# Half of a pairwise sum of attention exponentials moved from GpSimd to an accumulating DMA

## The chip, the cores and the metric

The kernel runs on one core of a Trainium2 chip. The metric is the device time of one execution in microseconds, lower is better. The engines named below are TensorE (PE, its weight loads PEld), VectorE (DVE), ScalarE (ACT), GpSimd (POOL) and SyncE (SP, which here only issues DMAs). The 16 DMA engines of the core move the data of every queue: of SP's, and of POOL's own queue.

## The reference

A post-norm decoder layer in float32, batch 2, 1024 tokens, width 512, 16 heads of 32: linear self-attention, then cross-attention to a context of 2048 rows, then a mixture of 8 experts (top 2). The change touches the softmax of the cross-attention alone:

```
q = (x1 @ wq.T)   -> [b, 16, 1024, 32]
k = (x2 @ wk.T)   -> [b, 16, 2048, 32]
v = (x2 @ wv.T)   -> [b, 16, 2048, 32]
dots = einsum('bhnd,bhmd->bhnm', q, k) * SCALE
attn = softmax(dots, axis=-1)
out  = einsum('bhnm,bhmd->bhnd', attn, v)
```

## The kernel before

There are three stages: the linear attention and the projections of the context (until about 570 us), the attention loop (until about 1530 us), and the experts. A plan, made in Python by `do(stage, key)`, is one list of units; every engine walks the list and carries out its own part of each unit, in that order, so the order of each engine's queue is the order of the plan.

**The loop.** A group is 4 heads (HG = 4) of one batch element. A turn is one group and one half of the queries (512); there are 16 turns. A turn walks the 2048 context rows in MT = 16 tiles of 128, two tiles at a time, so it has 8 pairs and the loop has 128. For each tile `s` and head `j`, TensorE multiplies keys and queries (`score`, L1194), ScalarE writes `exp` into `probs_of(t, s)[:, j, :]` (L1807). An exponential tile is 128 partitions x 4 heads x 512 queries, 8 KB in each partition. Even tiles lie in a ring of three buffers `probs_sum`, odd ones in a ring of three `probs_add`. The numerators (`num`, L1205) multiply both tiles with the values. For the denominators, the two tiles of a pair are first added, `a += b` with a in `probs_sum` and b in `probs_add` (`add_pair`, L1929 to L1936, POOL, one instruction for each head), and one multiplication with ones sums the result (`den`, L1223). Besides, each pair computes 8 tiles of scores for the row maxima of a later turn (L1175), which DVE reduces (L1468). The last 12 pairs are added by DVE (`by_vector`) and are not touched.

**The order in one pair.** The plan of a pair (L844 to L892, one `clock` each) is: the 8 scores of the next pair mixed with 8 maxima, some side work, `num` of both tiles, `den` of the pair before (it was put in `pending` with `clock + 1`), postponed divisions, then `add_pair`. So TensorE meets the `den` of a pair one whole pair after POOL was told to add it. `add_pair` waits for the last exponential of the odd tile and for the numerators of the even one. ScalarE, before it overwrites a buffer three pairs later, waits for its `num_summed`, and for `den_summed` (even tiles) or `pair_added` (odd tiles).

**Other traffic.** SP loads, during the loop, the keys of a later group in four chunks of three 256 KB transfers (`load_k`, L2070), queries (`load_q`, three of 256 KB), values (`load_v`, four of 256 KB), and stores and fetches rows of 1 MB at the end of a half. POOL also does the divisions by the denominators (`divide`, L1957) and, in the stage of the experts, gathers rows (L1968) and scatters results with an accumulating indirect DMA (`down`, L1977: 128 rows of 2 KB added to rows in DRAM, 256 KB in all).

Of the kernel before, what the change touches and what calls it, by code (L numbers as in the profile page):

```python
# [12 lines left out]
ALU = mybir.AluOpType  # L13
# [6 lines left out]
HG = P // DH  # L20
# [4 lines left out]
MT = M // P  # L25
# [95 lines left out]
def program(nc, t):  # L121
    ctx = ExitStack()
    with ctx:
        def signal(name, by=1):
            return Signal(Semaphore(ctx.enter_context(nc.semaphore(name))), by)

        def signals(name, n, by=1):
            return [signal(f"{name}{i}", by) for i in range(n)]

        def signals_on(name, n):  # L130
            on = Semaphore(ctx.enter_context(nc.semaphore(name)))
            return [Signal(on) for _ in range(n)]
# [16 lines left out]
        def bank(i):  # L149
            return pairs[i // 2][:, i % 2, :]  # L150
# [131 lines left out]
        def by_vector(t, s):  # L282

            return t == LAST or t == LAST - 1 and s >= HALF_TURN

        def chunk_of(b, mc):
            return B * NH + b * MCH + mc

# [34 lines left out]
        max_scored, max_taken = signal("max_scored"), signal("max_taken")  # L323
        top_taken, inverted = signals_on("tops_inverses", 2)
        top_hi, shift_copied = signals_on("shift_parts", 2)
        shift_turned = signal("shift_turned")
        scored, exp_done = signal("scored"), signal("exp_done")
        num_summed, num_copied = signal("num_summed"), signal("num_copied")
        pair_added, divided, top_lo = signals_on("pool_done", 3)
        last_pair_added = signal("last_pair_added")  # L330
        den_summed, den_copied = signal("den_summed"), signal("den_copied")
        counts_zero, folded = signals_on("fold_done", 2)
# [64 lines left out]
            "score": lambda t, s, j: (scored, exp_done),  # L397
            "num": lambda t, s: (num_summed,),
            "copy_num": lambda t: (num_copied,),
            "add_pair": lambda t, s: (last_pair_added if by_vector(t, s) else pair_added,),  # L400
            "den": lambda t, s: (den_summed,),
            "copy_den": lambda t: (den_copied,),
            "invert": lambda t, q: (inverted,),
# [180 lines left out]
        def context(b):  # L584
            for mc in range(MCH):
                m = chunk_of(b, mc)
                load_chunk(m + 2)
                for u in range(NG):
                    i = main_bank.next()
                    take_bank(("ctx_k", b, mc, u), i)  # L590
                    do("ctx_k_first", b, mc, u)
                    yield
                    do("ctx_k", b, mc, u)
                    yield
                    i = main_bank.next()
                    take_bank(("ctx_v", b, mc, u), i)
                    do("ctx_v_first", b, mc, u)
                    yield
                    do("ctx_v", b, mc, u)
                    split_chunk(m + 1, u)  # L600
                    yield
# [239 lines left out]
        for turn, (n, h) in enumerate(turns):  # L841
            b, g = groups[n]
# [51 lines left out]
        b, h = B - 1, NH - 1  # L894
        for k in range(HT):
# [1 line left out]
            do("rows_first", b, h, k)  # L897
        begin_parts(b, h)
        loop_end = (scored, num_summed, den_summed, exp_done, num_copied, den_copied, pair_added, last_pair_added,
                    max_taken, shift_copied, max_scored)  # L900
        gates["experts"] = [x.now() for x in loop_end]
        while divisions:
            invert(SHARE, 0)
# [112 lines left out]
        def probs_of(t, s):  # L1016

            tiles = probs[s % 2]
            return tiles[(t * MT + s) // 2 % len(tiles)]

        def probs_before(t, s):

            earlier_step = t * MT + s - 2 * len(probs[s % 2])
            return divmod(earlier_step, MT) if earlier_step >= 0 else None
# [4 lines left out]
        def _(_eng):  # L1029
            pe = Waits(nc.tensor)  # L1030

            def free_bank(*unit):
                if held_before[unit]:
                    pe.wait_ge(*emptied(held_before[unit]))
                return bank(bank_of[unit])
# [104 lines left out]
            def ctx_k_terms(b, mc, u):  # L1140
                return three_passes(columns(w_parts["k"], tile_of(u)), src_parts[chunk_of(b, mc) % 2])

            def ctx_k_first(b, mc, u):
                out = free_bank("ctx_k", b, mc, u)
                pe.wait_ge(*chunk_lo[chunk_of(b, mc), NC - 1])
                pe.wait_ge(*weight_lo["cv", NC - 1])
                terms = ctx_k_terms(b, mc, u)
                accumulate(out, terms[:len(terms) // 2], stop=False)
# [61 lines left out]
            def denominators_of(t, s):  # L1210
                if s == 1:
                    free_bank("den", t)
                tiles = [probs_of(t, s - 1)]
                if t == LAST and s == MT - 1:
                    tiles.append(probs_of(t, s))
                    pe.wait_ge(*exp_done[t, s, HG - 1])
                elif by_vector(t, s):
                    pe.wait_ge(*last_pair_added[t, s])
                else:
                    pe.wait_ge(*pair_added[t, s])  # L1220
                for tile in tiles:
                    for j in range(HG):
                        done = nc.tensor.matmul(bank(DEN)[j * DH:(j + 1) * DH, :], ones[:, 0:DH], tile[:, j, :],  # L1223
                                                start=s == 1, stop=s == MT - 1 and tile is tiles[-1])
                done.then_inc(den_summed.sem, 1)
# [72 lines left out]
            def down(e, i):  # L1298
# [3 lines left out]
                for f in range(NF):  # L1302
# [7 lines left out]
                    "turn_heads": turn_heads, "project": project, "turn_x1": turn_x1, "xq": xq,  # L1310
                    "ctx_k_first": ctx_k_first, "ctx_k": ctx_k, "ctx_v_first": ctx_v_first, "ctx_v": ctx_v,
                    "max": max_scores, "shift": shift, "score": score, "num": numerators, "den": denominators_of,
                    "rows_first": rows_first, "rows": rows, "parts_first": parts_first, "parts": parts,
                    "x1_logits": x1_logits, "fold": fold, "fold_turn": fold_turn, "logits": logits, "ranks": ranks,
# [388 lines left out]
        def _(_eng):  # L1703
            act, S = Waits(nc.scalar), nc.scalar
# [91 lines left out]
            def score(t, s, j):  # L1796
                act.wait_ge(*scored[t, s, j])
                if j == 0 and probs_before(t, s):
                    t0, s0 = probs_before(t, s)
                    act.wait_ge(*num_summed[t0, s0])  # L1800
                    if s0 % 2 == 0:
                        act.wait_ge(*den_summed[t0, s0 + 1])
                    elif by_vector(t0, s0):
                        act.wait_ge(*last_pair_added[t0, s0])
                    else:
                        act.wait_ge(*pair_added[t0, s0])
                S.activation(probs_of(t, s)[:, j, :], bank(bank_of["score", t, s, j]), ACT.Exp, scale=SCALE) \  # L1807
                    .then_inc(exp_done.sem, 1)

# [64 lines left out]
            def final(q):  # L1874
# [3 lines left out]
                for n in range(Q4):  # L1878
# [10 lines left out]
                    "split_chunk": split_chunk, "split_weight": split_weight, "keys": keys, "queries": queries,  # L1889
                    "turn_heads": turn_heads, "turn_x1": turn_x1, "xq": xq, "ctx_k": ctx_k, "ctx_v": ctx_v,  # L1890
                    "shift_high": shift_high, "shift": shift, "score": score, "copy_num": copy_num, "copy_den": copy_den, "x2": x2,
                    "x1_logits": x1_logits, "fold": fold, "parts": parts, "route_top": route_top, "turn_xe": turn_xe,
                    "split_w1": split_w1,
# [8 lines left out]
        def _(_eng):  # L1902
            pool, G = Waits(nc.gpsimd), nc.gpsimd
# [25 lines left out]
            def add_pair(t, s):  # L1929
                if not by_vector(t, s):  # L1930
                    a, b = probs_of(t, s - 1), probs_of(t, s)
                    pool.wait_ge(*exp_done[t, s, HG - 1])
                    pool.wait_ge(*num_summed[t, s - 1])
                    for j in range(HG):
                        done = G.tensor_tensor(a[:, j, :], a[:, j, :], b[:, j, :], ALU.add)  # L1935
                    done.then_inc(pair_added.sem, 1)  # L1936

# [34 lines left out]
            def down(e, i):  # L1972
                turn = e * NS + i
                pool.wait_ge(*eo_ready[e, i])
                if turn:
# [4 lines left out]

            here = {"gate_loop": pass_gate, "gate_second": pass_gate, "gate_experts": pass_gate, "gate_tail": pass_gate,
                    "load_consts": load_consts, "fetch_x": fetch_x, "shift_low": shift_low, "add_pair": add_pair,
                    "store_x1": store_x1, "divide": divide,
                    "gather": gather, "down": down}
# [244 lines left out]
```

## Time and profile before

| | us |
|---|---|
| median of 2 runs | 2080.24 (2080.16 to 2080.32) |
| the profiled execution's own time | 2077.41 |
| its span, first to last instruction | 2075.6 |
| busy: PE / DVE / ACT / POOL | 1931.0 / 1228.6 / 889.2 / 784.8 |
| first to last pair sum on POOL (L1935) | 570.1 to 1456.4 |

The span is 1.8 us shorter than the time of its own execution. A busy engine is not by itself the bound: what counts is which engine the others wait for at a given place, which the waits and the chain of a stretch tell. "issue" as a releaser is time in which an engine waited for nothing that the profile shows. The time from issue to landing of a DMA is counted from the start of the issuing instruction to the last update of its semaphore.

### The profile page before, as it was taken

What the parts mean: (1) busy time and instruction counts of PE and PEld (TensorE: products, weight loads), DVE (VectorE), ACT (ScalarE), POOL (GpSimd) and SP (SyncE); (2) the same over time, 40 slices, a digit from 0 to 9 for tenths busy, and PEclk for the clock granted to TensorE, in tenths of its full rate; (3) what the DMA queues carried; (4) which work ended last, traced back from release to release, by engine and by line L of the source; (5) the groups of instructions that cost most, each with busy time, mean ns of one, the idle gap of its engine ahead of it and who ended that gap; (6) DMA issues with size and microseconds to landing.
All of it is one profiled execution on the core that took longest, in us unless ns stands there. A gap on an engine that the chain in (4) does not pass through costs nothing.

```text
span 2075.6 us, 26469 instructions
## 1 busy us (share of the span) xinstructions
PE 1931.0 (93%) x10152; PEld 1270.0 (61%) x10152; DVE 1228.6 (59%) x2321; ACT 889.2 (43%) x1595; POOL 784.8 (38%) x675
## 2 busy tenths in 40 slices
PE   6999999999499999999999999999978999999991
PEld 5876666677355555555444544544438998888991
DVE  5565453157277777777767866877753444444434
ACT  3212322222265666656545545545734433333432
POOL 4002200000076777777656656756102222222110
PEclk9999999999799999999999999999988999999996
DMA  7002524574603122312424334332224444544315
GB/s 254 28 1 107 177 81 147 190 212 137 156 17 78 25 73 57 92 42 58 97 62 121 79 77 118 84 80 72 82 82 143 137 132 99 135 132 104 100 21 177
DMA packets 118942, 211.03 MB, mean 102 GB/s; under 512 B 10480, under 2 KB 28544, under 8 KB 118736
## 3 DMA queue, kind: packets, MB, share of 16 engines
q1 hardware_dynamic: 107264, 183.30, 30.0%
q0 software_dynamic: 9440, 21.86, 5.5%
q10 hardware_dynamic: 2112, 4.19, 0.5%
q8 instruction: 80, 1.31, 0.3%
q14 instruction: 46, 0.38, 0.1%
HBM read 147.15 MB, written 62.42 MB: 101 GB/s over the span
## 4 chain that ended last, share of the span: by engine, by line
PE 78%; DVE 13%; DMA 4%; ACT 2%; SPq 1%; issue 1%; POOL 0%; POOLq 0%; DVEq 0%; ACTq 0%
PE banks L1039 33%; PE banks L1205 11%; PE banks L1294 11%; PE banks L1175 9%; DVE max L1468 9%; PE banks L1194 7%; PE banks L1223 5%; PE banks L1045 2%; ACT probs_sum L1807 1%; DMA y_rows<-eo,tok 1%; DMA k_parts<-out_lo 1%; DMA wv_raw<-in_wv_t 1%; DMA bxo_cols<-in_bxo_cols 1%; DVE stats L1677 0%; DMA k_half<-in_xwk_t 0%
## 5 line engine op out<-in xcount | busy, mean ns | idle before, releaser
L1468 DVE TENSOR_REDUCE max<-banks 128x1 f32<-128x512 f32 x1024 | 628.1, 681 | 188.6 <-PE banks L1175 187.9
L1935 POOL TENSOR_TENSOR probs_sum<-probs_sum,probs_add 128x512 f32<-128x512 f32 x464 | 582.1, 1286 | 351.6 <-PE banks L1205 351.6
L1175 PE MATMUL banks<-k_stack,q_stack 98*128 98x512 f32 x1024 | 428.9, 426 | 30.4 <-DVE max L1468 30.0
L1807 ACT ACTIVATE probs_sum<-banks 128x512 f32<-128x512 f32 x512 | 264.9, 604 | 330.1 <-PE banks L1194 329.4
L1194 PE MATMUL banks<-q_stack,k_stack 98*128 98x512 f32 x1024 | 378.0, 400 | 15.2 <-ACT probs_add L1807 14.7
L1175 PEld LDWEIGHTS banks<-k_stack,q_stack 98*128 98x128 f32 x1024 | 192.3, 188 | 220.0 <-DVE max L1468 99.6
L1807 ACT ACTIVATE probs_add<-banks 128x512 f32<-128x512 f32 x512 | 271.7, 612 | 0.6 <-PE banks L1194 0.5
L1194 PEld LDWEIGHTS banks<-q_stack,k_stack 98*128 98x128 f32 x1024 | 192.4, 189 | 76.4 <-ACT probs_add L1807 26.0
L1977 POOL DMA_INDIRECT y_rows<-eo,tok x40 | 79.9, 1998 | 217.7 <-DVE eo L1667 163.6
L1205 PE MATMUL banks<-probs_sum,v_grp 128*32 128x512 f32 x1024 | 142.5, 618 | 0.0
L1205 PE MATMUL banks<-probs_add,v_grp 128*32 128x512 f32 x1024 | 139.5, 606 | 0.0
L1223 PE MATMUL banks<-probs_sum,ones 128*32 128x512 f32 x1024 | 137.4, 599 | 0.8 <-DVE probs_sum L1483 0.8
L1654 DVE TENSOR_TENSOR hid_lo<-hid,hid_hi 128x640 fp32r<-128x640 f32 x64 | 52.8, 825 | 142.5 <-ACT hid_hi L1872 142.5
L1039 PE MATMUL banks<-w_hi,hid_hi 128*128 128x512 f32 x320 | 128.6, 402 | 0.0
L1039 PE MATMUL banks<-w_hi,hid_lo 128*128 128x512 f32 x320 | 126.3, 395 | 0.0
L1039 PE MATMUL banks<-w_lo,hid_hi 128*128 128x512 f32 x320 | 125.8, 393 | 0.0
L1941 POOL TENSOR_TENSOR x_nat<-x_nat,bxo_row 128x512 f32<-128x512 f32 x16 | 21.1, 1350 | 267.7 <-PE banks L1045 267.7
L1294 PE MATMUL banks<-xe_hi,w_hi 128*128 128x320 f32 x512 | 117.6, 311 | 1.5 <-issue 1.5
L1294 PE MATMUL banks<-xe_lo,w_hi 128*128 128x320 f32 x512 | 117.3, 310 | 0.0
L1294 PE MATMUL banks<-xe_hi,w_lo 128*128 128x320 f32 x512 | 117.2, 310 | 0.0
L1867 ACT ACTIVATE hid<-banks,b1c 128x640 f32<-128x640 f32 x64 | 50.8, 794 | 137.0 <-PE banks L1294 135.0
L1664 DVE TENSOR_TENSOR eo<-banks,b2s 128x512 f32<-128x512 f32 x40 | 27.7, 691 | 126.6 <-PE banks L1039 117.9
(223 smaller groups left out, 2788.6 us busy)
## 6 DMA issues: line engine op xcount, KB each, us to landing
k_stack<-k_parts SPq DMA_DIRECT2D x144, 256.0 KB, 4.8
w_raw<-in_L_ffn_w SPq DMA_DIRECT2D x16, 2048.0 KB, 8.4
q_stack<-q_parts SPq DMA_DIRECT2D x48, 256.0 KB
v_grp<-v_rows SPq DMA_DIRECT2D x48, 256.0 KB, 3.1
raw<-in_ctx_t SPq DMA_DIRECT2D x8, 1024.0 KB, 6.5
k_parts<-out_hi SPq DMA_DIRECT2D x32, 256.0 KB, 2.5
k_parts<-out_lo SPq DMA_DIRECT2D x32, 256.0 KB, 2.9
v_rows<-pre SPq DMA_DIRECT2D x32, 256.0 KB, 2.3
```

Of the source, the lines that this page charges most:

```text
L1039: done = nc.tensor.matmul(out, lhsT, rhs, start=start and n == 0, stop=stop and n == len(operands) - 1)
L1175: nc.tensor.matmul(out, queries_of(t)[:, j, tile_of(k)], keys_of(t)[0:STK + SHIFT, j, mc * HALF:(mc + 1) * HALF], start=True, stop=True) \
L1194: nc.tensor.matmul(out, keys_of(t)[0:STK + SHIFT, j, tile_of(s)], queries_of(t)[:, j, :], start=True, stop=True).then_inc(scored.sem, 1)
L1205: done = nc.tensor.matmul(bank(NUM)[j * DH:(j + 1) * DH, :], v_grp[:, s, j * DH:(j + 1) * DH], probs_of(t, s)[:, j, :], start=s == 0, stop ...
L1223: done = nc.tensor.matmul(bank(DEN)[j * DH:(j + 1) * DH, :], ones[:, 0:DH], tile[:, j, :], start=s == 1, stop=s == MT - 1 and tile is tile ...
L1294: done = nc.tensor.matmul(pairs[first][:, h, 0:HC], w, x[:, h * HC:(h + 1) * HC], start=n == 0, stop=n == len(terms) - 1)
L1468: V.reduce_max(max4[:, tiles_of(t), :, :][:, k, j, mc:mc + 1], bank(bank_of["max", t, mc, k, j]), AX.X) \
L1654: V.tensor_tensor(hid_lo[:, f, :], hid[f % 2][:, :], hid_hi[:, f, :].bitcast(F32), ALU.subtract) \
L1807: S.activation(probs_of(t, s)[:, j, :], bank(bank_of["score", t, s, j]), ACT.Exp, scale=SCALE) \
L1867: S.activation(hid[f % 2][:, :].rearrange("p (h n) -> p h n", h=2), pairs[first][:, :, 0:HC], ACT.Gelu, bias=b1c[:, e, f:f + 1]).then_inc( ...
L1935: done = G.tensor_tensor(a[:, j, :], a[:, j, :], b[:, j, :], ALU.add)
L1977: G.indirect_dma_start(out=y_rows, in_=eo[turn % EO][:, :], in_offset=None, compute_op=ALU.add, out_offset=bass.IndirectOffsetOnAxis(ap=to ...
```

## The change

For the pairs that POOL sums, heads 2 and 3 are added by one DMA issued from POOL's queue with `accum_op=add`, from tile b to tile a (128 partitions x 4 KB, 512 KB), ahead of the two additions that POOL still makes for heads 0 and 1. The DMA counts up one of three new semaphores. TensorE (ahead of `den`) and ScalarE (ahead of overwriting b) wait for it beside `pair_added`.

```diff
+        def sum_tile(t, s):
+
+            return (t * MT + s) // 2 % 3
...
+        pair_summed = signals("pair_summed", 3, 16)
...
-            "add_pair": lambda t, s: (last_pair_added if by_vector(t, s) else pair_added,),
+            "add_pair": lambda t, s: (last_pair_added,) if by_vector(t, s) else (pair_added, pair_summed[sum_tile(t, s)]),
...
         loop_end = (scored, num_summed, den_summed, exp_done, num_copied, den_copied, pair_added, last_pair_added,
-                    max_taken, shift_copied, max_scored)
+                    max_taken, shift_copied, max_scored, *pair_summed)
...
                     pe.wait_ge(*pair_added[t, s])
+                    pe.wait_ge(*pair_summed[sum_tile(t, s)][t, s])
...
                         act.wait_ge(*pair_added[t0, s0])
+                        act.wait_ge(*pair_summed[sum_tile(t0, s0)][t0, s0])
...
                     pool.wait_ge(*num_summed[t, s - 1])
-                    for j in range(HG):
+                    G.dma_start(a[:, HG // 2:, :], b[:, HG // 2:, :], accum_op=ALU.add) \
+                        .then_inc(pair_summed[sum_tile(t, s)].sem, 16)
+                    for j in range(HG // 2):
                         done = G.tensor_tensor(a[:, j, :], a[:, j, :], b[:, j, :], ALU.add)
                     done.then_inc(pair_added.sem, 1)
```

## Rows read from the trace of the kernel before

**Rows 1.** Busy time by stretch: busy (x instructions) by engine, PE clock, DMA share, GB/s

```profile
700.00:750.00 50.00, 49.90 (x292) 26.09 (x290) 38.84 (x66) 31.51 (x64) 38.54 (x35) 1.00 0.16 39
900.00:1000.00 100.00, 99.80 (x588) 51.48 (x590) 79.27 (x136) 62.78 (x127) 75.80 (x67) 1.00 0.18 42
1000.00:1100.00 100.00, 95.83 (x501) 45.02 (x493) 68.31 (x127) 50.00 (x98) 58.99 (x52) 0.98 0.35 80
1200.00:1300.00 100.00, 94.90 (x506) 44.10 (x504) 68.56 (x146) 51.05 (x100) 58.90 (x52) 0.97 0.39 97
```

**Rows 2.** Chain of waits, 800 to 860 us, shares by line

```profile
by line: PE banks L1175 29.1%; PE banks L1205 27.8%; PE banks L1194 23.7%; PE banks L1223 12.9%; DVE max L1468 6.2%; PE banks L1183 0.5%; issue 0.1%
```

**Rows 3.** Waits, 576 to 1457 us, of PE (first two) and POOL: total, times, longest

```profile
PE banks L1194 <- ACT probs_add L1807: 14.7, 15, 2.9
PE banks L1183 <- DVE max L1468: 3.6, 2, 2.0
...
POOL probs_sum L1935 <- PE banks L1205: 280.4, 115, 6.0
```

**Rows 4.** The line L1935: duration ns min/median/max, first and last start

```profile
L1935 POOL TENSOR_TENSOR probs_sum<-probs_sum,probs_add x464: 1267/1286/1303, 570.1 to 1456.4; 128x512 f32<-128x512 f32 x155
```

**Rows 5.** Timeline of two pairs: start us, us, instruction, idle before

```profile
1000.08 5.02 POOL L1935 TENSOR_TENSOR probs_sum<-probs_sum,probs_add 128x512 f32<-128x512 f32 x4 [1.77 <-PE banks L1205]
...
1000.57 1.04 PE L1223 MATMUL banks<-probs_sum,ones 128*32 128x512 f32 x8
...
1006.53 1.04 PE L1205 MATMUL banks<-probs_add,v_grp 128*32 128x512 f32 x8
...
1006.89 5.02 POOL L1935 TENSOR_TENSOR probs_sum<-probs_sum,probs_add 128x512 f32<-128x512 f32 x4 [1.37 <-PE banks L1205]
1006.96 0.13 PEld L1223 LDWEIGHTS banks<-probs_sum,ones 128*32 128x32 f32 x4 [0.30 <-issue]
1007.39 1.04 PE L1223 MATMUL banks<-probs_sum,ones 128*32 128x512 f32 x8
...
1012.30 1.27 SPq L2078 DMA_DIRECT2D k_stack<-k_parts  x3
...
1013.71 5.01 POOL L1935 TENSOR_TENSOR probs_sum<-probs_sum,probs_add 128x512 f32<-128x512 f32 x4 [1.79 <-PE banks L1205]
```

**Rows 6.** The scatter L1977: duration ns, waits for it, and time to landing

```profile
L1977 POOL DMA_INDIRECT y_rows<-eo,tok x40: 1552/2070/2475, 1605.6 to 2035.1; - x40
...
  POOL y_rows L1977: 49.4, 8
...
DMA to landing us min/median/max: 4.5/5.3/10.7
```

**Rows 7.** POOL's plain DMA issues at the start, and one scatter by stretches

```profile
8.61 0.60 POOL L1915 DMA_DIRECT2D x_rows<-in_zeros  x1
...
2028.84:2030.40 1.56, 1.56 (x8) 1.28 (x7) 0.00 (x0) 0.00 (x0) 1.55 (x1) 1.00 0.01 5
2030.40:2030.97 0.57, 0.57 (x4) 0.46 (x3) 0.00 (x0) 0.00 (x0) 0.00 (x0) 1.00 0.00 0
2030.97:2033.22 2.25, 1.71 (x8) 1.04 (x6) 0.50 (x1) 0.00 (x0) 0.00 (x0) 1.00 0.91 117
2033.22:2033.56 0.34, 0.00 (x0) 0.00 (x0) 0.30 (x2) 0.00 (x0) 0.00 (x0) 1.00 0.00 0
```

**Rows 8.** DMA queues: packets, MB, share of 16 engines' span

```profile
q1 hardware_dynamic: 107264, 183.30, 30.0%
q0 software_dynamic: 9440, 21.86, 5.5%
```

**Rows 9.** Stretches of one pair each, and one key load (959 to 963 us)

```profile
700.00:706.81 6.81, 6.81 (x42) 3.44 (x41) 5.55 (x10) 4.28 (x9) 5.43 (x6) 1.00 0.00 0
959.00:963.00 4.00, 4.00 (x27) 2.11 (x20) 2.16 (x4) 2.53 (x6) 4.00 (x4) 1.00 0.74 177
1000.00:1006.81 6.81, 6.81 (x44) 3.44 (x40) 5.32 (x10) 4.05 (x8) 5.45 (x5) 1.00 0.99 217
1013.62:1020.43 6.81, 6.71 (x35) 3.53 (x28) 4.87 (x9) 4.65 (x9) 5.01 (x4) 1.00 0.49 112
```

**Rows 10.** Key loads L2078: duration ns of an issue, time to landing

```profile
L2078 SPq DMA_DIRECT2D k_stack<-k_parts x144: 302/432/1707, 412.9 to 1409.3; - x144
...
DMA to landing us min/median/max: 3.6/4.8/14.6
```

## Prediction

> **What bounds the kernel now.** I read the busy times by stretch first, because a share over the span mixes three stages. Inside the attention loop TensorE is busy 99.8 of 100 us where a turn is undisturbed, and still 95 where row work is woven in, while POOL has 59 to 77 [rows 1]. The chain of waits of a quiet stretch is TensorE's for 93.5%, the rest DVE's maxima; POOL has no share [rows 2]. The waits say the same from the other side: in the whole stretch of pair sums TensorE waits 14.7 us for ScalarE and 3.6 us for DVE, never for POOL, and POOL waits 280.4 us for TensorE, in 115 of its 116 pairs [rows 3]. The timeline of two pairs gives the period, 1006.89 - 1000.08 = 6.81 us, and POOL's sum takes 5.02 of them [rows 5]. So the change relieves an engine that is off the path. The question is only whether the new transfer lands before TensorE asks for it.
>
> **What is removed.** Two of four additions in each of 116 pairs (464 / 4), 1.286 us each: 2.57 us a pair, 298 us of POOL's busy time [rows 4]. What it covers is TensorE's work, which goes on as before, so it is worth 0. A gain that reaches the end would have to come out of TensorE's idle time: 4.2 and 5.1 us in 100 in the disturbed stretches and 0.2 in the quiet ones [rows 1], an estimated 20 to 25 us from 650 to 1457 us, and none of it is a wait for POOL [rows 3]. Divisions stand behind the sums in POOL's queue and come 5.0 - 3.6 = 1.4 us earlier; nothing on TensorE waits for them, so 0 again.
>
> **What is added on POOL.** One DMA issue a pair. A plain one took 0.60 us [rows 7], an accumulating indirect one 1.55 to 2.48 us [rows 6]. I take 1.0 us: the pattern is plain, as in the first row, but each partition needs a second read. Ends 0.6 and 2.5 us. POOL then has about 1.0 + 2.57 = 3.6 us a pair (at worst 5.1, as now), its own sum is still ready in time. The issue comes first in its queue and holds no wait, so what is queued behind it (two additions, divisions, the low part of the shifts) is later by nothing against today. The pair sums on POOL last 1267 to 1303 ns without exception while DVE reduces maxima beside them [rows 4]. The Trainium skill (SBUF — State Buffer, section "SBUF: two separate sides", the "DVE blocks DMA" trap) says that an operation of VectorE that uses both ports keeps GpSimd from writing descriptors, so that a DMA of its queue starts late; the narrow spread of the additions speaks for no such lock in the loop, and by that rule the issue would move toward the long end of the range above.
>
> **The deadline.** The issue starts where POOL's sum starts now, at 1000.08. TensorE's denominator matmuls of that pair start at 1007.39, their weight loads at 1006.96 [rows 5]. So a landing within about 7.1 us costs nothing. Each stall also moves the next deadline back by its own length, since the next issue is made ahead of the stalled matmul; the cost of a pair is only what its landing exceeds 7.1 us plus the stall before it. Queued behind a waiting denominator on TensorE are the scores of the next-but-one pair and the maxima, hence ScalarE and DVE. The two added waits of ScalarE cost 0: for the even buffer of the same pair it already waits for the denominators, which come after the sum.
>
> **The landing.** The trace has no transfer between tiles on chip, so I bound its four pieces by the scatter. Issue: 1.0 (0.6 to 2.5), as above. Issue end to first data: 2030.97 - 2030.40 = 0.57 us; last data to semaphore 0.34 us [rows 7]. Data: the scatter of 256 KB into DRAM takes 2.25 us [rows 7], so 512 KB take 4.5 us if the rate stays; that is the upper end. At the lower end, the plain queue spends 0.300 x 16 x 2075.6 / 183.3 = 54 engine-us on a MB [rows 8], 1.8 us for 0.524 MB over 16 engines. The queue of gathers and scatters together spends 0.055 x 16 x 2075.6 / 21.86 = 84, 2.7 us. I take 3.2 us, between 2.7 and 4.5: the read of the destination stays, the start in DRAM goes. Sum 1.0 + 0.57 + 3.2 + 0.34 = **5.1 us**, with ends 0.6 + 0.57 + 1.8 + 0.34 = 3.3 and 2.5 + 0.57 + 4.5 + 0.34 = 7.9 us. In a quiet pair 5.1 is hidden by 2 us.
>
> The Trainium skill (DMA: Bandwidth & Descriptors, section on the anatomy of one DMA) fits a DMA of this queue as 2.0 us plus its bytes at 436 GB/s, 3.2 us here; and Collectives: The Full Stack (on why ReduceScatter is half of AllGather) says that an add in a DMA costs a second source read, which makes it 4.4 us. The fit gives 2.6 us for the 256 KB scatter, and its best landing is 4.5 us [rows 6], so the trace does not agree and I go by rows; by the rule the sum would be no stall anywhere.
>
> **Other traffic.** A quiet pair has no DMA at all, but one with a key load has the 16 engines 49% busy and one with keys and queries 99% [rows 9]. A key load is issued 1.4 us before the pair sum (1012.30 against 1013.71) [rows 5] and lands 4.8 us after its issue in the median [rows 10], so its data meets the first 2 to 2.5 us of ours; at its share of 0.74 [rows 9] that adds up to 1.9 us: 5.1 + 1.9 = 7.0, just inside. About 40 pairs have one by the plan (11 groups of four chunks, less the last ones, which meet DVE's sums). Some 16 pairs (13 query loads, the ends of three halves) have queries or row blocks too and keep the engines full for most of the pair. There the delay can be as for the 8 scatters of 40 that POOL waited for, of which the slowest took 10.7 against 5.3 us [rows 6]. I take 3 us in those: 5.1 + 3 - 7.1 = 1.0, but in about half of them TensorE has row work between and the deadline is later: 8 x 1.0 = **8 us**. The transfers delayed by ours (keys, queries, values) are wanted pairs or turns later: 0. TensorE's clock fell to a mean of 0.97 in stretches with 5 us of idle time [rows 1]; a few stalls of 1 us could add one or two us more, which I leave in the range.
>
> **Sum.** 0 - 0 + 0 + 8 on the profiled execution's 2077.4 gives 2085 us; the median shown is 2.8 us higher, so 2080.2 + 8 = **2088 us**.
>
> **Rivals.**
>
> *A, slower: the landing itself passes the deadline.* It decides from 7.1 us on. At the rate and issue of the scatter, 2.1 + 0.57 + 4.5 + 0.34 = 7.5 us; a mean pair lasts (1456.4 - 570.1) / 115 = 7.7 us [rows 4], so about 70 pairs have the short period and pay 0.4 us, 28 us, and the 40 with a key load pay up to 1.9 more, 76: +104, **2184 us**. At the far end of 7.9 us it is +136. For it: the only accumulate in the trace is that slow, and sums on chip may be no better. Against: it goes to DRAM, with addresses from a table.
>
> *B, slower: the landing is fine alone, but other transfers stand ahead in the DMA engines.* If a key load costs ours 4 us, three quarters of the 10.7 - 5.3 = 5.4 us that the slowest scatter lost [rows 6], then 5.1 + 4 - 7.1 = 2.0 us in about 40 pairs: +80, **2160 us**. Against: a key load is 0.75 MB, the weight load beside those scatters 2 MB.
>
> *C, nothing at all:* the landing is 4.5 us or less and every stall disappears: **2080 us**.
>
> *D, faster:* a shorter queue on POOL lets ScalarE or DVE run ahead. At most TensorE's idle 20 to 25 us: **2058 us**, still not 2%. No wait that it would end is named [rows 3].
>
> *E, it does not relieve POOL:* the issue takes 2.5 us, as long as the additions that it replaces. Time as in A or the forecast; it is in A's chance.
>
> **How the numbers follow.** Forecast 0.42, C 0.20, A 0.24, B 0.12, D 0.02. Two per cent, about what a measurement of this kernel can tell from no change, is 41.6 us: the forecast, C and D are inside, A and B beyond. So slower 0.36, same 0.62, faster 0.02. The forecast's own range is 2078 to 2120. For 8 in 10 it must hold most of A and B: low 2076 (C less a few us), high 2190, which leaves out A's far end and most of D.
>
> **What would show it.** In the changed profile: L1935 at 232 instructions of 1.29 us and POOL some 180 us less busy; a POOL issue of about 1 us and a landing near 5 us, min to max 4 to 9; TensorE's period still 6.81 us in 900 to 1000 us, its waits for the DMA on L1223 about 8 us in all, and these beside key and query loads alone. Rival A shows as a wait in quiet pairs and a period over 6.81; B as waits of 2 us beside loads alone. I am wrong if the median landing is over 7 us or if TensorE's waits for it exceed 40 us.

## The result and the profile after

The changed kernel takes 2118.91 us (median of 2, 2116.08 to 2121.74) against 2080.24: ratio 1.0179, 95% interval 1.0162 to 1.0195. That is 38.7 us slower, just inside the 2% that count as no change. The profiled execution took 2121.74 us, its span 2119.9.

Where the forecast was right comes first. The line of the new issue and the waits of TensorE, in the profile after (the columns are those of [rows 3] and [rows 6]):

```profile
L1941 POOL DMA_DIRECT2D probs_sum<-probs_add x116: 865/872/933, 574.0 to 1499.5; - x116
...
  PE banks L1229: 26.2, 9
DMA to landing us min/median/max: 4.5/6.1/12.2
```
```profile
PE banks L1229 <- DMA probs_sum<-probs_add: 26.2, 9, 4.1
PE banks L1199 <- ACT probs_add L1814: 12.8, 14, 2.6
```

TensorE now waits for the transfer that sums two heads: 9 times, 26.2 us, at most 4.1. Its waits for ScalarE are about as before (14.7 us in 15 [rows 3]). POOL's busy time fell from 784.8 to 602.0 us. Quiet pairs are as forecast. Busy time by stretch, columns as in [rows 1]:

```profile
700.00:750.00 50.00, 49.90 (x302) 25.17 (x294) 38.54 (x67) 29.39 (x60) 26.85 (x28) 1.00 0.48 99
900.00:1000.00 100.00, 96.17 (x559) 49.19 (x558) 74.23 (x128) 59.24 (x118) 49.98 (x50) 0.98 0.58 120
```

From 700 to 750 us TensorE is 49.90 of 50 busy, exactly as before, though the DMA engines went from 16% to 48%. From 900 to 1000 us it has lost 3.6 us. Landings of single stretches of the same line tell the two apart. The first lines are six quiet pairs, the next one a pair with a key load, the last one a pair with keys and queries.

```profile
L1941 POOL DMA_DIRECT2D probs_sum<-probs_add x6: 865/876/880, 694.1 to 728.6; - x6
DMA to landing us min/median/max: 4.5/4.5/4.6
...
L1941 POOL DMA_DIRECT2D probs_sum<-probs_add x1: 865/865/865, 749.0 to 749.0; - x1
DMA to landing us min/median/max: 6.5/6.5/6.5
...
L1941 POOL DMA_DIRECT2D probs_sum<-probs_add x1: 882/882/882, 904.0 to 904.0; - x1
DMA to landing us min/median/max: 10.7/10.7/10.7
```

The nine sums that TensorE waited for landed after 8.3 to 12.2 us. Six of them are in pairs with a query load, three beside row blocks of 1 MB. The timeline of a pair with queries shows the whole loss (start us, us, instruction, idle before):

```profile
1017.68 0.98 SPq L2087 DMA_DIRECT2D k_stack<-k_parts  x2
...
1018.70 1.38 SPq L2098 DMA_DIRECT2D q_stack<-q_parts  x3
...
1019.13 0.88 POOL L1941 DMA_DIRECT2D probs_sum<-probs_add  x1 [3.35 <-PE banks L1210]
...
1025.19 1.04 PE L1210 MATMUL banks<-probs_add,v_grp 128*32 128x512 f32 x8
...
1029.29 1.93 PE L1229 MATMUL banks<-probs_sum,ones 128*32 128x512 f32 x8 [3.06 <-DMA probs_sum<-probs_add]
1031.15 0.80 PE L1180 MATMUL banks<-k_stack,q_stack 98*128 98x512 f32 x1
```

The keys and queries are issued just ahead of the sum; the denominators, due at 1026.2, start at 1029.29 after 3.06 us of idle time. And then they take 1.93 us for the 1.04 of [rows 5], because TensorE's clock has fallen. These are the stretches right behind the waits of 3.06 and 1.4 us. The last three numbers of a row are the granted clock, the DMA share and GB/s:

```profile
1029.29:1036.20 6.91, 6.91 (x21) 4.20 (x22) 3.55 (x6) 2.76 (x5) 0.04 (x1) 0.53 0.47 113
798.70:805.50 6.80, 6.76 (x40) 3.50 (x44) 4.88 (x8) 4.05 (x8) 1.79 (x3) 1.00 1.01 269
```

Here 21 matmuls fit where 40 do at full clock: at 0.53 nearly the whole stretch ran at 1.2 GHz. Stretches behind the six waits of 3 us or more had 0.53, 0.75, 0.53, 0.75, 0.60 and 0.55; behind the three of 1.4 to 2.2 us, 1.00.

What the loss is made of is read between the first and the last pair sum, in the kernel before (first row) and in the changed one (second row):

```profile
570.10:1456.40 886.30, 864.77 (x4867) 435.48 (x4859) 664.20 (x1246) 502.51 (x1000) 605.91 (x531) 0.99 0.30 72
574.00:1499.50 925.50, 880.30 (x4850) 443.33 (x4846) 661.92 (x1243) 502.85 (x996) 419.40 (x413) 0.97 0.62 134
```

This part is 39.2 us longer. TensorE is idle 23.7 us more: 26.2 us of waits for the sum, less 2.5 us that it no longer waits for ScalarE and DVE. And it is busy 15.5 us more with the same matmuls, which is the clock. So the loss is waits and clock in about the ratio of three to two. The span as a whole grew by 44.3 us. Of the other 5.1, 3.9 lie ahead of the first sum, where TensorE waits 26 to 27 us for DVE in both kernels and runs at 1.2 GHz for some us behind it. That lasted longer in the profile of the changed kernel (again before, then changed):

```profile
570.00:575.00 5.00, 5.00 (x28) 2.92 (x24) 3.81 (x7) 3.58 (x8) 4.93 (x4) 1.00 0.00 0
570.00:575.00 5.00, 5.00 (x20) 1.26 (x18) 1.50 (x3) 1.53 (x3) 0.96 (x2) 0.50 0.00 0
```

No sum of the DMA is waited for there, and why this part differs is not shown.

### The profile page after: what moved, and what is told of

Read it like the earlier page. It is cut to its first block, busy times and chain, and to the rows that moved or that the text cites. A ratio compares the mean times of both kernels' runs of the same rounds, so it can differ in the third digit from the quotient of the medians.

```text
span 2119.9 us, 26561 instructions
## 1 busy us (share of the span) xinstructions
PE 1951.1 (92%) x10152; PEld 1281.1 (60%) x10152; DVE 1228.0 (58%) x2321; ACT 891.6 (42%) x1595; POOL 602.0 (28%) x559
## 4 chain that ended last, share of the span: by engine, by line
PE 75%; DVE 12%; DMA 8%; ACT 2%; SPq 1%; issue 1%; POOL 0%; POOLq 0%; ACTq 0%; DVEq 0%
PE banks L1044 33%; PE banks L1300 11%; PE banks L1210 10%; PE banks L1180 8%; DVE max L1474 7%; PE banks L1199 7%; PE banks L1229 5%; DMA probs_sum<-probs_add 4%; PE banks L1050 1%; ACT probs_sum L1814 1%; DMA k_parts<-out_lo 1%; DMA wv_raw<-in_wv_t 1%; DMA bxo_cols<-in_bxo_cols 1%; DVE stats L1683 0%; DMA y_rows<-eo,tok 0%
## 5 line engine op out<-in xcount | busy, mean ns | idle before, releaser
L1180 PE MATMUL banks<-k_stack,q_stack 98*128 98x512 f32 x1024 | 436.8, 434 | 29.9 <-DVE max L1474 28.9
L1199 PE MATMUL banks<-q_stack,k_stack 98*128 98x512 f32 x1024 | 386.0, 408 | 13.3 <-ACT probs_add L1814 12.8
L1180 PEld LDWEIGHTS banks<-k_stack,q_stack 98*128 98x128 f32 x1024 | 197.9, 193 | 225.0 <-issue 95.8
L1944 POOL TENSOR_TENSOR probs_sum<-probs_sum,probs_add 128x512 f32<-128x512 f32 x232 | 327.7, 1580 | 0.0
L1941 POOL DMA_DIRECT2D probs_sum<-probs_add x116 | 101.3, 873 | 579.2 <-PE banks L1210 573.9
L1199 PEld LDWEIGHTS banks<-q_stack,k_stack 98*128 98x128 f32 x1024 | 197.6, 194 | 74.4 <-ACT probs_add L1814 23.9
L1229 PE MATMUL banks<-probs_sum,ones 128*32 128x512 f32 x1024 | 142.2, 619 | 27.0 <-DMA probs_sum<-probs_add 26.2
L1874 ACT ACTIVATE hid<-banks,b1c 128x640 f32<-128x640 f32 x64 | 50.8, 794 | 137.0 <-PE banks L1300 137.0
```

Source lines behind the costliest of these rows:

```text
L1180: nc.tensor.matmul(out, queries_of(t)[:, j, tile_of(k)], keys_of(t)[0:STK + SHIFT, j, mc * HALF:(mc + 1) * HALF], start=True, stop=True) \
L1199: nc.tensor.matmul(out, keys_of(t)[0:STK + SHIFT, j, tile_of(s)], queries_of(t)[:, j, :], start=True, stop=True).then_inc(scored.sem, 1)
L1941: G.dma_start(a[:, HG // 2:, :], b[:, HG // 2:, :], accum_op=ALU.add) \
```

## The experiments

Each ratio is against the kernel before, timed on the same chip. Two theories stood against each other: W, waits for late landings and the clock behind them; T, the traffic itself costs time.

**Queries apart, first attempt.** The last key chunk and the query load of a pair are in different places of the plan.

```diff
-            if s == MT - 1:
-                load_q(t + PLACES)
+            if s == 1 and t - 1 + PLACES < len(turns):
+                do("load_q_first", t - 1 + PLACES)
+            if s == 5 and t and t - 1 + PLACES < len(turns):
+                do("load_q_rest", t - 1 + PLACES)
```

> The changed kernel, but the four transfers of a query load are no longer issued in the same pair as the last key chunk: two of them one pair later, two three pairs later, each beside a value chunk alone. Theory W (the changed kernel loses its time in pairs in which keys and queries fill the DMA engines, so that the sum lands after 10 to 12 us and TensorE waits, and TensorE's clock falls to 1.2 GHz behind such a wait): the landings over 10 us disappear, a maximum near 8, and the time goes back to 2085 to 2092 us. Rival T (the traffic of the sum costs time by itself, through the memory that TensorE, DVE and POOL also use, as the longer additions on POOL suggest): the traffic is the same, so the time stays at 2115 to 2122 us.

Measured 2120.31 us, ratio 1.0184 (1.0166 to 1.0201). No gain, as T has it, but the edit did not do what it says. SP's timeline:

```profile
670.82 1.28 SPq L2090 DMA_DIRECT2D k_stack<-k_parts  x3
672.15 0.91 SPq L2101 DMA_DIRECT2D q_stack<-q_parts  x2
```

Nothing in SP's queue holds the query load back to the later pair, so its first two transfers are issued right behind the keys all the same; the other two followed at 680.18. A place in the plan is a time only for an engine that waits for something there. TensorE waited 29.0 us in 16. The run tells nothing between W and T, and was made again below.

**Not beside queries.** `with_dma(t, s)` is false for the last two pairs of a turn; there POOL adds four heads.

```diff
+            return s not in (MT - 3, MT - 1)
...
+                    if with_dma(t, s):
...
-                    for j in range(HG // 2):
+                    for j in range(HG // 2 if with_dma(t, s) else HG):
```

> The changed kernel, but in the last two pairs of each turn (in which the query load runs) POOL adds all four heads and there is no accumulating DMA; about 87 of 116 pairs keep it. Theory W: 2082 to 2090 us, since the pairs with the waits are the ones left out. Rival T: three quarters of the traffic remain, so three quarters of the loss, about 2108 us.

Measured 2090.02 us, ratio 1.0038 (1.0022 to 1.0055). A quarter of the transfers carried three quarters of the loss: W. TensorE's waits for the DMA are down to 6.7 us in 3.

**One head.**

```diff
-                    G.dma_start(a[:, HG // 2:, :], b[:, HG // 2:, :], accum_op=ALU.add) \
+                    G.dma_start(a[:, HG - 1:, :], b[:, HG - 1:, :], accum_op=ALU.add) \
...
-                    for j in range(HG // 2):
+                    for j in range(HG - 1):
```

> The changed kernel, but the DMA sums one head (256 KB) and POOL three. Theory W: the data part of the quiet landing halves, 4.5 to about 3.1 us, that of the worst pairs from 10 to 12 us to 8 to 10, so stalls of 3 to 4 us become 1 to 2 us in 10 pairs and the time is 2090 to 2100 us. Rival T: half the traffic, half the loss, 2099 us; the two come close here, the landing tells the size of the data part.

Measured 2112.13 us, ratio 1.0146 (1.0126 to 1.0166), more than either theory said. Landings, and the waits:

```profile
  PE banks L1229: 17.5, 9
DMA to landing us min/median/max: 3.3/4.8/10.8
```

Half the bytes take 1.2 us off the quiet landing (4.5 to 3.3) and 1.4 off the worst (12.2 to 10.8). So the delay does not grow with our bytes, and halving the transfer hardly helps. The packet records of the changed kernel's trace tell where the delay arises. In a quiet pair the first packet of POOL's queue starts 1.44 us after the issue; for the nine sums that were waited for it starts after 3.5 to 6.3 us, and from there to the landing it is 4.8 to 6.6 us in place of 3.1. A little over half of the delay is thus ahead of our first packet, and the rest falls while the packets are served.

All six waits of 2.1 to 2.9 us cost clock as well here. The row begins right behind the longest of them:

```profile
917.90:925.00 7.10, 7.10 (x23) 4.94 (x16) 4.15 (x6) 3.76 (x7) 0.90 (x1) 0.52 0.06 11
```

The clock records of all the runs with a wait for the sum say: behind each of the 37 such waits of 2.7 us or more, or from within it on, TensorE ran at 1.2 GHz for some us. So it did behind 12 of the 23 waits between 1.9 and 2.7 us, and behind one of the 37 between 0.9 and 1.9 us.

**The traffic alone.** POOL adds four heads; in every second pair a DMA of nearly the same size goes from b into a tile that nobody reads, and TensorE does not wait for it (ScalarE does, before it overwrites b).

```diff
+                        G.dma_start(scratch[:, :, :], b[:, HG // 2:, :SCRATCH], accum_op=ALU.add) \
+                            .then_inc(pair_summed[0].sem, 16)
+                    for j in range(HG):
```

> The kernel before (POOL adds all four heads), and in every second pair, the ones with the query loads among them, an accumulating DMA of the same size (4000 of 4096 B in each partition) from the same tile b into a tile that nobody reads; TensorE waits for none of them. Theory W: there is no wait, so 2080 us, within 4. Rival T: half of the traffic of the changed kernel is there, so half its loss, 2095 to 2102 us. The additions on POOL that follow such a DMA show whether its issue alone makes them longer.

Measured 2120.51 us, ratio 1.0195 (1.0176 to 1.0214). This spoke against W, and neither theory had it so large. The stretches show that it is another loss:

```profile
900.00:1000.00 100.00, 99.80 (x594) 51.06 (x587) 77.34 (x133) 61.05 (x124) 85.88 (x77) 1.00 0.42 87
...
1100.00:1200.00 100.00, 86.58 (x470) 45.69 (x469) 81.41 (x153) 49.03 (x97) 65.35 (x58) 0.90 0.51 116
```

Where there is no row work, TensorE loses nothing at all. Where there is, look at DVE, and at POOL beside it:

```profile
1155.30 0.88 POOL L1980 TENSOR_TENSOR heads_t<-num_c,den_c 128x128 f32<-128x128 f32 x1
1155.96 5.08 POOL L1958 TENSOR_TENSOR probs_sum<-probs_sum,probs_add 128x512 f32<-128x512 f32 x4
...
1155.84 5.23 DVE L1598 TENSOR_TENSOR col_s<-weight 128x4 f32<-128x4 f32 x1
1161.11 0.17 DVE L1599 TENSOR_SCALAR col_s<-col_s 128x4 f32<-128x4 f32 x1
```

An addition of 4 numbers in each partition, of two operands on chip, takes 5.23 us and ends when POOL's four additions end; its neighbours take 0.17. Meanwhile TensorE waited 5.0 us for DVE's maxima. Here POOL carries both the issue (1.20 us) and four additions, so its sums reach into the slots of such DVE operations. In the loop 22 of them are more than 0.4 us over their shortest time, 33.8 us in all; there are 4 in the kernel before, 3.5 us in all, and 1 in the changed one. The Trainium skill (SBUF — State Buffer, section "SBUF: two separate sides") has it that such an operation and one of GpSimd that reads SBUF exclude each other for a whole instruction; this trace agrees, and DVE stood behind four of them in a row. The experiment had two causes in it. The next one leaves this one out.

**No wait, two heads.** As above, but POOL adds heads 0 and 1 alone in every pair; the sums of heads 2 and 3 are left out of the denominators.

```diff
-                    for j in range(HG):
+                    for j in range(HG // 2):
```

> As the run with the traffic alone (every second pair, the ones with the query loads among them, a 500 KB accumulating DMA into a tile that nobody reads, TensorE waits for none), but POOL adds only heads 0 and 1 in every pair, so its queue is as short as in the changed kernel; the pair sums of heads 2 and 3 are left out of the denominators. Theory W: no wait for the DMA, and POOL is not busy when DVE's small operations with two operands in SBUF come, as it was in that run: 2080 us, within 4. Rival T: at least half of the loss, 2098 us or more. If the loss of 39 us stays, it is the DMA's issue on POOL that costs, and not the landing.

Measured 2079.97 us, ratio 0.9993 (0.9983 to 1.0002). The landings are as late as in the changed kernel:

```profile
L1955 POOL DMA_DIRECT2D scratch<-probs_add x58: 1179/1202/1281, 577.5 to 1448.8; - x58
...
DMA to landing us min/median/max: 4.9/6.5/12.1
```

and nobody waits. T is refuted as far as this traffic goes: half of the transfers, the ones beside the query loads among them, cost nothing. The loss of the run before is gone too, with POOL's additions of heads 2 and 3. What costs in the changed kernel is the wait.

**Queries held.** The first attempt again, with waits that make SP keep the place.

```diff
             def load_q_first(t):
+                sp.wait_ge(*scored[t + 1 - PLACES, 1, HG - 1])
                 load_q(t, slice(0, 2))
...
             def load_q_rest(t):
+                sp.wait_ge(*scored[t + 1 - PLACES, 5, HG - 1])
                 load_q(t, slice(2, 4))
```

> The changed kernel with the query loads really taken apart from the key loads: SP holds the first two of the four transfers until the scores of the next pair have started to be made (a wait on scored), and the other two until two pairs later. In the attempt before, SP ran ahead of the plan and issued them right behind the key chunk. Theory W (waits for sums that land late beside long loads, and TensorE's clock behind them): the landings near 10 us go except beside row blocks, the time is 2086 to 2096 us. Rival T (traffic by itself): 2115 to 2122 us as before.

Measured 2096.99 us, ratio 1.0076 (1.0053 to 1.01). Moving thirteen loads by one to three pairs takes back more than half of the loss; the time is 1 us above what W said. 7 waits, 13.1 us, are left, and the four long ones among them (1.8 to 4.1 us, landings of 8.8 to 12.2 us) are beside row blocks. The same edit on the kernel before is the control.

> Control: the kernel before (no accumulating DMA) with the query loads held back as in the run that took them off the key loads. Both theories: 2080 us, within 4; if it is slower, part of what that run still loses is due to the later queries and not to the sums.

Measured 2080.57 us, ratio 1.0005 (0.9995 to 1.0014): the later queries cost nothing.

**Four heads.** The DMA sums the whole tile, POOL nothing, and nobody waits for POOL.

```diff
-                    G.dma_start(a[:, HG // 2:, :], b[:, HG // 2:, :], accum_op=ALU.add) \
+                    G.dma_start(a[:, :, :], b[:, :, :], accum_op=ALU.add) \
...
-                    for j in range(HG // 2):
-                        done = G.tensor_tensor(a[:, j, :], a[:, j, :], b[:, j, :], ALU.add)
-                    done.then_inc(pair_added.sem, 1)
```

> The DMA sums all four heads (1 MB a pair), POOL none. Theory W with the sizes read from the changed kernel: issue 0.87, 0.57 to the first packet, data 2 x 2.75 = 5.5, 0.33 to the semaphore, so a quiet landing of 7.3 us against a deadline of 6.9: 0.4 us in some 60 short pairs, 2.5 to 3 us in the 35 with key loads, 6 to 7 in the 10 with queries; +110 to +190 us with the clock: 2190 to 2270 us. Rival T: twice the traffic, twice the loss, 2158 us, and no waits in quiet pairs.

Measured 2214.46 us, ratio 1.0654 (1.0616 to 1.0692).

```profile
  PE banks L1228: 92.5, 54
DMA to landing us min/median/max: 6.9/9.0/13.8
```

The quiet landing is 6.9 us (7.3 expected), at the deadline; the total is inside W's range, and there are waits in quiet pairs too, as W said.

**DMA last.** The two additions ahead of the issue.

```diff
-                    G.dma_start(a[:, HG // 2:, :], ...
                     for j in range(HG // 2):
                         done = G.tensor_tensor(a[:, j, :], a[:, j, :], b[:, j, :], ALU.add)
                     done.then_inc(pair_added.sem, 1)
+                    G.dma_start(a[:, HG // 2:, :], ...
```

> The changed kernel with POOL's two additions ahead of the DMA issue instead of behind it; the same work and traffic, issued about 2.5 us later. Theory W: what is left to the deadline falls from 6.9 to 4.4 us; quiet landings (4.5) pay 0.1 us, those beside key loads (6.5) 2 us in some 35 pairs, those beside values up to 1.5, the worst 6: +120 to +170 us, 2200 to 2250 us. Rival T: the same traffic, 2119 us.

Measured 2148.09 us, ratio 1.0307 (1.0279 to 1.0334): slower with the same work and traffic, which T does not allow, but half of what W said.

```profile
  PE banks L1229: 43.9, 19
DMA to landing us min/median/max: 4.5/4.6/11.1
```

The median landing fell from 6.1 to 4.6 us. The issue is 2.1 us later: it stands 2.5 us behind the start of POOL's additions, and these start 0.4 us earlier than the issue did. A sum beside a key load then finds that load nearly done, so fewer sums are late than W had counted. What delays a sum is the work issued shortly ahead of it.

**Loads behind the sum.** Queries apart, and every key, query and value load waits for the landing of its pair's sum; then the row blocks too.

```diff
+            def hold(t, s):
+                sp.wait_ge(*pair_summed[sum_tile(t, s)][t, s])
...
+                while deferred:
+                    do("hold", turn, s + 1)
+                    do(*deferred.pop(0))
```

> The changed kernel with queries apart, and every key, query and value load of the loop issued only after the accumulating DMA of its pair has landed, so that a sum is not queued behind loads that were issued a little earlier. If what makes a landing late is the load issued ahead of it (the first packet comes late), sums beside key loads land after 4.5 to 5.8 us in place of 6.5, landings over 6.9 us remain only beside row blocks, and the time is 2084 to 2092 us. If what counts is the sum of traffic in a pair whatever its order, the landings stay near 6.5 and the time near the 2097 us of the run with queries apart.

Measured 2091.96 us, ratio 1.0056 (1.0025 to 1.0088). The median landing went to 5.5 us as expected of the order of issue. But 14 waits, 13.1 us in all, remain. I had expected late landings beside row blocks only, and most of these sums are beside keys or queries. A load issued at the landing of one sum falls close to the issue of the next: the loads beside these late sums were issued from 2.5 us before the sum to 1.7 us behind it. The interval overlaps that of the run with queries held, so holding keys and values as well is not shown to gain.

> As the run with loads behind the sum, and the fetches and stores of row blocks (1 MB each) as well. By the same reasoning the last late landings shrink but do not all go, since a block of 1 to 2 MB runs into the next pair's sum: 2081 to 2089 us, 2 to 5 us below the run without it. It can not be below 2080: TensorE is the bound and does the same work.

Measured 2109.73 us, ratio 1.0139 (1.0122 to 1.0156); my expectation was wrong. Blocks of 1 to 2 MB released together with the loads meet the following sums (12 waits, 19.3 us, the longest 4.0). Their own places were better.

**The account.** For each run, TensorE's waits for the DMA are added to half of what it ran at 1.2 GHz beyond the kernel before, and the sum is set against the difference in span (2075.6 us before). A mean granted clock c over a span means 2 x (1 - c) x span at 1.2 GHz: 124.5 us before, 173.8 in the changed kernel. Half of the difference is lost work, an estimate, since idle time at 1.2 GHz loses none. The clock is given to 0.001, which is 2 us in the second column. The last column is the same half for the loop alone, from the trace's clock records: what lies between the long stretches at 1.2 GHz (27 us or more) that every run has ahead of the loop and behind it.

| kernel | waits | half the extra time at 1.2 GHz | sum | span above before | of the second, in the loop |
|---|---|---|---|---|---|
| changed | 26.2 | 24.6 | 50.8 | 44.3 | 18.8 |
| queries apart, first attempt | 29.0 | 20.5 | 49.5 | 45.0 | 18.8 |
| one head | 17.5 | 22.3 | 39.8 | 38.0 | 11.9 |
| queries held | 13.1 | 6.9 | 20.0 | 18.5 | 3.4 |
| not beside queries | 6.7 | 4.6 | 11.3 | 13.5 | 5.1 |
| loads behind the sum | 13.1 | 4.7 | 17.8 | 18.0 | 0.0 |
| rows too | 19.3 | 11.5 | 30.8 | 32.5 | 8.5 |
| DMA last | 43.9 | 30.1 | 74.0 | 72.2 | 29.0 |
| four heads | 92.5 | 32.6 | 125.1 | 130.8 | 30.7 |
| no wait, two heads | 0 | 0.1 | 0.1 | 1.4 | -1.7 |
| before, queries held | 0 | 6.3 | 6.3 | 1.3 | -1.7 |

Eleven kernels from 1 to 131 us are accounted for within 7 us. The last row has no DMA sum at all, and still 6.3 us in the second column, all of it outside the loop. So the second column carries some us that have nothing to do with the sums, up to 10 in the run with one head, and where it is 7 us or less it tells little. The run with the traffic alone is left out, because what TensorE waits for there is DVE and ScalarE: 44.0 us in the loop, for 18.3 before.

## Why the prediction was right, and where it was not

**The bound and the sign were right.** TensorE bounds the loop, relieving POOL gained nothing, and no version that makes all the sums came in below the kernel before. The 2118.91 us lie in my range and inside the forecast's own, 2078 to 2120, but 31 us above the point. The loss is 38.7 us for 8, and 1 us more would have left the forecast's own range, so that it held was luck.

**The landing was right.** Three stretches of a quiet pair, from its issue at 707.76, show it in pieces: ahead of the data, the data, and behind it.

```profile
707.76:709.18 1.42, 1.42 (x14) 0.44 (x7) 0.53 (x2) 0.00 (x0) 1.42 (x2) 1.00 0.00 0
709.18:711.96 2.78, 2.78 (x13) 1.96 (x12) 2.60 (x5) 2.37 (x5) 2.42 (x3) 1.00 0.99 189
711.96:712.30 0.34, 0.34 (x3) 0.23 (x2) 0.34 (x1) 0.34 (x2) 0.00 (x0) 1.00 0.00 0
```

The issue took 0.87 us for the 1.0 taken, 0.55 for 0.57 passed from its end to the data, the data took 2.78 for 3.2, and 0.34 for 0.34 the rest. The quiet landing is 4.5 us for 5.1, within its bounds of 3.3 and 7.9. Of the two estimates that the prediction set aside, 3.2 us was too low and 4.4 us nearer than its own. The deadline, a landing less the wait for it, is 6.9 us after the issue for 7.1. Beside a key load 6.5 us, so 2.0 more for the 1.9 taken, and just hidden. Rival A was refuted by the quiet pairs; E by POOL's 183 us less. Doubling the scatter's data time would have been too high, and the rate of the whole software queue (2.7 us) came near. Going from one to two heads adds 1.2 us, from two to four 2.4. Whether the scatter is slower for its indirect addresses or for its target in DRAM is not shown.

**The step that failed** is "I take 3 us in those: 5.1 + 3 - 7.1 = 1.0 [...] 8 x 1.0 = 8 us", the pairs with queries and row blocks. The number of pairs that pay was right, 8 taken and 9 measured, and of the 12 sums that landed after more than 8 us three cost nothing, because TensorE was late for another reason: row work in one, a wait for ScalarE in another, the slower clock behind the wait of the pair before in the third. The delay was mis-sized: the slowest scatter had lost 5.4 us, and I took 3. The nine landings measured are 8.3 to 12.2 us, 3.8 to 7.7 more than a quiet one, and the waits 1.4 to 4.1: 26.2 us in place of 8. The cause is rival B's, other transfers issued ahead (queries held took back more than half with the same sums), but confined to those pairs; B had put it at the 40 pairs with key loads, which were hidden.

**The second term was left in the range.** I gave the clock "one or two us more"; it cost 15.5 in the loop. Rows 1 had shown 0.97 with scattered idle time, but all six waits of 3 us and more brought 1.2 GHz behind them. Stalls of the 1 us that I had taken would hardly have: in all runs one wait under 1.9 us did.

**POOL's additions** became 1.58 us in the mean from 1.29, but two together take 2.82, so the records overlap; TensorE's matmuls did not wait for it. By my own signs the forecast was not wrong, with a median landing of 6.1 us for 7 and 26.2 us of waits for 40. But the longest landing was 12.2 us for the 9 that I had named.

## What to carry to other kernels

A transfer with a deadline is to be judged by the busiest pair and not by the median one: here 107 of 116 sums were free and 9 cost everything. A DMA is served late behind what was issued shortly before it, so here it was cheaper to move the background load (holding 13 loads took back 22 us) than to make the urgent transfer smaller (half the bytes took back about 7). Count the clock behind a wait of TensorE as well: here 26.2 us of waits brought 15.5 us of slower work, nearly all behind the waits of 3 us or more. And when the engine that is relieved is not the bound, all this only buys back a loss. Denominators taken one pair later, which would give each sum 6.8 us more, were not tried.

## What the runs showed of the hardware beyond what was expected

- An accumulating DMA between tiles on chip has a landing of 3.3, 4.5 and 6.9 us for 256, 512 and 1024 KB, alone: 2.1 us and 1.2 us for each 256 KB. Its issue takes POOL 0.87 us whatever the size in these three; with rows of 2000 B for each head (the runs with a tile nobody reads) it took 1.20 us.
- With the DMA engines at 48% in place of 16%, TensorE was 49.90 of 50 us busy as before: no contention for the memory was seen.
- A tiny DVE addition with both operands on chip stood for 5.23 us behind four additions of POOL, while DVE's maxima, one operand from PSUM, ran 0.68 us beside them undisturbed.
